# Layer-norm, attention and routed experts on one core: experts as one part between samples 15 and 16, dispatch and gathers inside the samples

## The reference

```
xn = _layernorm(x, axis=-1)
qkv = jnp.einsum('bsm,qhdm->bqhsd', x, W_qkv)           # 16 heads of 64
qk_rot = qk * cos + _rotate_half(qk) * sin               # first 32 of 64 dims
attn = softmax(where(causal, -inf, scores) / sqrt(DK))
probs = softmax(x @ router_w + router_b); top 2 of 9     # the ninth is a skip
h = gelu(einsum('btd,edf->ebtf', x, w1)); y = einsum('ebtf,efd->ebtd', h, w2)
x + attention(xn) + experts(xn)
```

## Time and profile before

| | |
|---|---|
| median of 3 runs | 1595.74 us (1595.12 to 1598.11) |
| span of the profiled execution | 1591.3 us |
| granted TensorE clock, mean | 0.924 |
| busy: PE, DVE, ACT, POOL | 1262.6, 1119.9, 1129.0, 985.1 us |

### The profile page before, as it was taken

One profiled execution on the slowest core, in us unless ns is written; L12 is line 12 of the kernel. 1 busy time (PEld: TensorE's weight loads), 2 busy tenths in 40 slices (PEclk: granted clock), 3 DMA queues, 4 the chain that ended last, 5 costly groups with the idle time before them and its releaser, 6 DMA issues.

```text
span 1591.3 us, 47515 instructions
## 1 busy us (share of the span) xinstructions
PE 1262.6 (79%) x13412; PEld 899.4 (57%) x13413; DVE 1119.9 (70%) x4292; ACT 1129.0 (71%) x3645; POOL 985.1 (62%) x1635
## 2 busy tenths in 40 slices
PE   2417989999899999999899999999859999567620
PEld 1304656666566666666566666666539899445520
DVE  5687787788877887788877887787647777345441
ACT  6407888888888888888888888888758888234310
POOL 3306888778877888778877888778640000544555
PEclk9658999999999999999999999999979999688765
DMA  9612233322332233322332233322422333222242
GB/s 288 166 39 56 61 76 89 74 62 60 87 89 62 62 69 88 81 62 60 85 87 65 61 67 86 83 64 60 115 81 81 84 88 86 66 79 76 75 132 65
DMA packets 121888, 131.83 MB, mean 83 GB/s; under 512 B 11568, under 2 KB 81456, under 8 KB 121520
## 3 DMA queue, kind: packets, MB, share of 16 engines
q1 hardware_dynamic: 113200, 113.41, 29.3%
q0 software_dynamic: 8576, 17.33, 3.8%
HBM read 29.89 MB, written 33.69 MB: 40 GB/s over the span
## 4 chain that ended last, share of the span: by engine, by line
PE 27%; POOL 20%; issue 19%; DVE 13%; DMA 10%; ACT 7%; DVEq 2%; another core or an unknown queue 1%; POOLq 0%; ACTq 0%; SPq 0%
DMA sorted_x_dram<-send_x,send_at 9%; PE bank L1056 6%; PE bank L1057 6%; PE bank L1058 6%; POOL probs L450 5%; POOL probs L451 4%; POOL arena L433 4%; ACT probs L597 3%; POOL arena L438 3%; PE bank L1127 2%; PE bank L1137 2%; PE bank L1151 2%; POOL arena L432 2%; PE bank L1186 1%; POOL sorted_x_dram L455 1%
## 5 line engine op out<-in xcount | busy, mean ns | idle before, releaser
L597 ACT ACTIVATE probs<-arena,neg_max 128x128 f32<-128x128 f32 (+1 forms) x1024 | 453.2, 446 | 94.7 <-DVE neg_max L910 77.3
L450 POOL TENSOR_TENSOR probs<-probs,inv_total 128x128 f32<-128x128 f32 x512 | 207.0, 404 | 184.8 <-DVE inv_total L917 127.9
L910 DVE CUSTOM_DVE_ANT_0 arena<-bank,causal 128x128 f32<-128x128 f32 (+1 forms) x1024 | 317.4, 348 | 0.0
L500 POOL DMA_INDIRECT arena<-sorted_y_dram,slots x128 | 123.3, 964 | 275.6 <-DMA sorted_y_dram<-arena 171.2
L1137 PE MATMUL bank<-ident,probs 128*128 128x128 f32 x1536 | 265.2, 282 | 13.0 <-POOL probs L451 4.7
L451 POOL TENSOR_SCALAR probs<-probs,inv_total 128x256 f32<-128x256 f32 x512 | 246.4, 481 | 0.0
L1137 PEld LDWEIGHTS bank<-ident,probs 128*128 128x128 f32 x1536 | 174.1, 142 | 83.5 <-issue 51.8
L597 ACT ACTIVATION_READ_ACCUMULATOR probs<-arena,neg_max 128x1 f32 x1024 | 195.2, 191 | 0.0
L578 ACT ACTIVATE probsT<-bank 128x384 f32<-128x384 f32 x384 | 184.4, 480 | 2.3 <-PE bank L1137 2.2
L928 DVE TENSOR_TENSOR arena<-bank,arena 128x256 f16<-128x256 f32 x256 | 107.3, 419 | 110.9 <-ACT arena L583 88.9
L1056 PE MATMUL bank<-xnT_lo,wqk_hi 128*128 (+1 forms) x512 | 143.7, 281 | 39.3 <-DVE arena L875 28.4
(11 more groups left out here) (155 smaller groups left out, 3378.5 us busy)
## 6 DMA issues: line engine op xcount, KB each, us to landing
second<-arena SPq DMA_DIRECT2D x128, 256.0 KB, 4.3
arena<-arena SPq DMA_DIRECT2D x128, 256.0 KB, 4.3
arena<-sorted_x_dram SPq DMA_DIRECT2D x80, 128.0 KB
sorted_y_dram<-arena SPq DMA_DIRECT2D x80, 128.0 KB
sorted_x_dram<-arena SPq DMA_DIRECT2D x3, 2560.0 KB, 20.1
arena<-experts_dram SPq DMA_DIRECT2D x8, 512.0 KB, 4.4
out_dram<-acc SPq DMA_DIRECT2D x16, 256.0 KB
sorted_x_dram<-arena SPq DMA_DIRECT2D x1, 2624.0 KB, 21.2
```

The source lines that it names most:

```text
L450: nc.gpsimd.tensor_tensor(p0, p0, inv_total[:, s % 4, 0:1].broadcast_to([P, P]), ALU.mult)
L597: last = nc.scalar.activation(probs[:, s % 4, at:at + w], masked[:, s % 2, at:at + w], ACT.Exp, bias=neg_max[:, s % 2, t:t + 1], scale=-1. ...
L910: last = nc.vector.tensor_tensor_reduce(out=masked[:, s % 2, at:at + w], in0=SC[s % 2][:, at:at + w], in1=causal[:, at:at + w], scale=1.0, ...
```

## The change

The sorted buffer has one part: 72 expert tiles instead of 80. The experts run between samples 15 and 16. Samples 0 to 15 send four tiles each (`PER`), by eight sends in steps `SEND_AT`, each still ahead of a wait for the one before; samples 16 to 31 gather and add the results of four tiles each (two of an earlier sample, two of their own), by eight gathers in steps `GATHER_AT` into a ring of four buffers (`stage`) and eight `combine`s in steps `COMBINE_AT`, and store two finished pairs of tiles each. The low parts of the rotary queries are taken on VectorE (`rope_low`), as those of the keys. Four of the eight experts' weights are loaded and split in the head (high parts on ScalarE, low parts on GpSimd by a scaling and a subtraction each), the other four around the end of sample 15. The owners of the expert tiles are found by one comparison and one sum instead of 14 small operations. Every engine's program now has two loops of samples with the expert loop between them. The core of the diff:

```diff
-PARTS = (44, 20)
+MID = B // 2
+PER = NT // MID
+EARLY = 4
 
 ET = 2 * P
-MAX_T = max(PARTS) * P // ET
-PART_T = [TOP * n * P // ET + E for n in PARTS]
-TILES = sum(PART_T)
-NS = E * len(PARTS)
+MAX_T = NT * P // ET
+TILES = TOP * NT * P // ET + E
...
-COMBINE_AT = PART_T[0] // BODY
-COMBINED = (0, 2, 2, 2)
-RING = sum(COMBINED)
+BACKS = 4
...
-SEND_AT = [1, 9, 12, 14]
+SEND_AT = [1, 3, 5, 7, 9, 11, 12, 14]
+GATHER_AT = [1, 3, 5, 7, 9, 10, 11, 13]
+COMBINE_AT = [3, 5, 7, 9, 11, 12, 13, 15]
...
+OPENING, FORMER, TURN, REOPEN, LATTER, FINAL = range(6)
+FILLS = (OPENING, REOPEN)
...
+        def former_samples(eng, body):
+
+
+            body(0, 0, OPENING)
+            with eng.Fori(0, MID // 2 - 1) as i:
+                body(2 * i + 1, 1, FORMER)
+                body(2 * i + 2, 0, FORMER)
+            body(MID - 1, 1, TURN)
+
+        def latter_samples(eng, body):
+
+            body(MID, 0, REOPEN)
+            with eng.Fori(MID // 2, B // 2 - 1) as i:
+                body(2 * i + 1, 1, LATTER)
+                body(2 * i + 2, 0, LATTER)
...
+            for e in range(EARLY):
+                load_expert(e)
...
+                if at == TURN:
+                    for r in range(GRP):
+                        sp.wait_ge(q_stacked[r], STACKED * (b + 2))
+                        sp.wait_ge(k_stacked[r], STACKED * (b + 2))
+                    for e in range(EARLY, E):
+                        load_expert(e)
+                if at in (REOPEN, LATTER, FINAL):
+                    store_former(b)
+                if at in (LATTER, FINAL):
...
+            def store_former(b):
+
+                u = b - MID
+                sp.wait_ge(combined, TOP * PER * u + TOP * TPS)
+                tiles_at = slice(TPS * u, TPS * u + TPS) if isinstance(u, int) else bass.ds(TPS * u, TPS)
+                sp.dma_start(out_tiles[:, tiles_at, :], acc[:, tiles_at, :]).then_inc(stored, 16)
...
-            def q_rope_low(j, m):
-                pool.wait_ge(rope_hi, ROPES * m + j + 1)
-                hi, lo = parts("rope", j)
-                nc.gpsimd.tensor_tensor(lo, roped[j], hi, ALU.subtract).then_inc(q_rope_lo, 1)
...
+            for e in range(EARLY):
+                pool.wait_ge(raw_hi, 4 + e)
+                nc.gpsimd.tensor_scalar(raw_e[e], raw_e[e], W_SCALE, 1.0, ALU.mult, ALU.mult).then_inc(early_scaled, 1)
+            for e in range(EARLY):
+                pool.wait_ge(early_scaled, e + 1)
+                nc.gpsimd.tensor_tensor(w_lo[:, e, :, :], raw_e[e].rearrange("p (k f) -> p k f", k=2), w_hi[:, e, :, :],
+                                        ALU.subtract).then_inc(early_low, 1)
...
+            def gather(k):
+
+                nc.gpsimd.indirect_dma_start(
+                    out=stage[:, k % BACKS, :], out_offset=None, in_=sorted_y[0:ROWS, :],
+                    in_offset=bass.IndirectOffsetOnAxis(ap=rows_at[:, k:k + 1], axis=0)).then_inc(gathered[k % BACKS], 16)
+
+            def sample(b, parity, at):
                 for s in range(H):
-                    if not first and s in SEND_AT:
-                        i = SEND_AT.index(s)
-                        if i == 0:
-                            pool.wait_ge(send_ready, b)
-                        else:
-                            pool.wait_ge(sent, 16 * (TPS * TOP * (b - 1) + i))
-                    if not (first and s < INV_LAG):
+                    sends = at in (OPENING, FORMER, TURN) and s in SEND_AT
+                    gathers = at in (REOPEN, LATTER, FINAL) and s in GATHER_AT
+                    if sends and s == SEND_AT[0]:
+                        pool.wait_ge(send_ready, b + 1)
+                    elif sends:
+                        pool.wait_ge(sent, 16 * (PER * TOP * b + SEND_AT.index(s)))
+                    if gathers:
+                        u, k = b - MID, GATHER_AT.index(s)
+                        if k == 0:
+                            pool.wait_ge(rows_ready, u + 1)
+                        if not (at == REOPEN and k < BACKS):
+                            pool.wait_ge(combined, TOP * PER * u + k - BACKS + 1)
+                    if not (at in FILLS and s < INV_LAG):
                         scale(16 * b + s - INV_LAG, s - INV_LAG)
-                    for kind, j, u, psum, n in beside(b, first, last, s - 3):
-                        if kind == "rope" and j < 2:
-                            q_rope_low(j, b + 1)
-                    for kind, j, u, psum, n in beside(b, first, last, s - 1):
+                    for kind, j, u, psum, n in beside(b, at, s - 1):
                         if kind == "rope":
                             rope_add(j, b + 1)
-                    if not first and s in SEND_AT:
+                    if sends:
                         send(SEND_AT.index(s))
...
+                    if gathers:
+                        gather(GATHER_AT.index(s))
...
+            former_samples(pool, sample)
+            rest_of(MID - 1)
+            for done in ys_out:
+                pool.wait_ge(done, 16 * TILES // 2)
+            latter_samples(pool, sample)
+            rest_of(B - 1)
...
+                if at == OPENING:
+                    act.wait_ge(early_low, EARLY)
...
+            former_samples(act, sample)
+            act.wait_ge(s_ready, 8 * MID)
+            for e in range(EARLY, E):
                 split_high(e)
+            rest_of(MID - 1)
 
             def xs_part(i, k):
...
-                step(nc.vector.memset(owner_f[0:1, :], 0.0))
-                for e in range(1, E):
-                    for h in range(len(PARTS)):
-                        own = owner_f[0:1, h * PART_T[0]:h * PART_T[0] + PART_T[h]]
-                        last = nc.vector.scalar_tensor_tensor(own, grid[0:1, 0:PART_T[h]], first_tile[0:1, e, h:h + 1], own,
-                                                              ALU.is_ge, ALU.add)
-                    step(last)
+                reached = scan[0][0:1, 0:TILES * (E - 1)].rearrange("p (n e) -> p n e", e=E - 1)
+                step(nc.vector.tensor_tensor(reached, grid[0:1, :].unsqueeze(2).broadcast_to([1, TILES, E - 1]),
+                                             first_tile[0:1, 1:E].unsqueeze(1).broadcast_to([1, TILES, E - 1]), ALU.is_ge))
+                step(nc.vector.reduce_sum(owner_f[0:1, :], reached, axis=AX.X))
...
             def dispatch(b):
 
                 if not (isinstance(b, int) and b == 0):
-                    dve.wait_ge(sent, 16 * TPS * TOP * b)
+                    dve.wait_ge(sent, 16 * PER * TOP * b)
+                for t in range(PER):
+                    tile = b * PER + t
+                    nc.vector.tensor_scalar(stage[:, t, :], row(acc, tile), row(neg_mean[:].unsqueeze(2), tile),
+                                            row(rstd[:].unsqueeze(2), tile), ALU.add, ALU.mult)
+                nc.vector.tensor_copy(rows_at[:].rearrange("p (t n) -> p t n", n=TOP), tile_slots(b * PER, PER)).then_inc(send_ready, 1)
+
+            def call_rows(b, at):
+
+                if at == REOPEN:
+                    dve.wait_ge(sent, 16 * TOP * NT)
+                former, own = (rows_at[:, 4 * i:4 * i + 4].rearrange("p (t n) -> p t n", n=TOP) for i in range(2))
+                nc.vector.tensor_copy(former, tile_slots((b - MID) * TPS, TPS))
+                nc.vector.tensor_copy(own, tile_slots(b * TPS, TPS)).then_inc(rows_ready, 1)
+
+            def combine(b, k):
+
+                u = b - MID
+                tile, n = (TPS * u if k < 4 else TPS * b) + k % 4 // TOP, k % TOP
+                dve.wait_ge(gathered[k % BACKS], 32 * u + 16 * (k // BACKS) + 16)
+                if n > 0:
+                    dve.wait_ge(combined, TOP * PER * u + k)
+                elif k >= 4:
+                    dve.wait_ge(mixed, b + 1)
+                a = row(acc, tile)
+                nc.vector.scalar_tensor_tensor(a, stage[:, k % BACKS, :], row(gates, tile)[:, n:n + 1], a,
+                                               ALU.mult, ALU.add).then_inc(combined, 1)
+
+            def mix(b):
+
                 for t in range(TPS):
                     tile = b * TPS + t
-                    if isinstance(tile, int):
...
-            def k_rope_low(j, m):
+            def rope_low(j, m):
                 dve.wait_ge(rope_hi, ROPES * m + j + 1)
                 hi, lo = parts("rope", j)
-                nc.vector.tensor_tensor(lo, roped[j % 2], hi, ALU.subtract).then_inc(k_rope_lo, 1)
+                nc.vector.tensor_tensor(lo, roped[j % 2], hi, ALU.subtract).then_inc(q_rope_lo if j < 2 else k_rope_lo, 1)
 
...
-                            k_rope_low(j, b + 1)
-                    if not (first and s < O_LAG) and (s - O_LAG) % 2 == 1:
+                            y_add(b - 1, j, u, psum, at in (FORMER, TURN))
+                    for kind, j, u, psum, n in beside(b, at, s - 3):
+                        if kind == "rope":
+                            rope_low(j, b + 1)
...
+                    if at in (OPENING, FORMER, TURN):
+                        if s == 0:
```

(29 more changed lines are left out.)

442 lines of the change are left out of this document (178 added, 264 removed).

## The result

The changed kernel takes 1608.4 us (median of 8 runs, 1598.8 to 1614.6) against 1595.95 us, ratio 1.0076 with a 95% interval of 1.0054 to 1.0099: 0.8% slower, where 3.5% faster was forecast. Its profiled execution took 1614.56 us with a span of 1612.7.

The account below looks back on a forecast made before the run. Bounds: GpSimd and VectorE in the rotary part, TensorE and equally long sends in the second, gathers at the end. From 1591.3 us, mainly -175.3 for experts, +93.4 and +22 for samples: 1537.4, with 4.4 to the median 1541.8; range 1490 to 1590.

Parts of the forecast that it names:

- 151 + 68 us more than the tiles need: Last two stretches of the kernel before: time spent beyond the tiles' own need, with tiles beside gathers taking 6.0 us.
- The saving of 175.3 us: Expert stage: eight tiles fewer and none beside a gather, 228.1 us in place of 403.4.
- Experts: Expert stage: 72 tiles at 3.04 us with GpSimd idle, handover down from 10.9 to 5.0 us.
- Samples 0 to 15: Eight sends instead of four: rotary part +1.4 us, second part +4.4, so 38.5 us a sample; +93.4 over sixteen.
- the chain of landings: Second part of samples 0 to 15: one more send waiting for a landing, +3.9 us, with `dispatch` +4.4, not hidden.
- Samples 16 to 31: Eight gathers and combines: 34.3 us a sample, bounds 32 and 38; VectorE waits about 1.5 us for step 9's gather.
- Meetings of GpSimd and VectorE: Samples 16 to 31: VectorE held up by GpSimd instructions at ten new meetings, 0.7 us a sample altogether.
- lock-out rival: Samples 16 to 31: the engines lock each other out, 0.8 us at each of ten meetings, 1657 us; chance 8%.
- The moved subtractions: Rotary part: two subtractions of 1.16 us leave GpSimd and come to VectorE at 0.69 us each.
- Ends: Sample 31 stays at 40.4 us plus 3 for the last store; the drain after sample 15 adds 7.7.
- Hidden sends: Rival: extra sends hide, samples 0 to 15 cost 1 us more each rather than 5.8, 1463 us; chance 12%.
- The clock did fall: Rival: TensorE's clock falls; at 0.65 its work would take 46 us a sample, 1660 us; chance 3%.

Follow-up runs that it names:

- x_after_p120: Changed kernel with 120 idle memsets at VectorE's start and 110 between the sample loops: 1575.1 us, 0.989 of the kernel before.
- x_scratch: Changed kernel with a sample's eight sends going to eight DRAM tensors, none waiting for another: 1543.2 us, 0.968 of the kernel before.
- x_after_again: Changed kernel without an edit, run again beside a kernel before of 1526.8 us: 1603.8 us, ratio 1.050.
- x_qlow_pool: Changed kernel with q's two rotary low parts moved back from VectorE to GpSimd: 1637.5 us, 1.027 of the kernel before.

## Why the prediction was wrong

The change made the kernel 0.8% slower where 3.5% faster was forecast. The mechanisms that the forecast named are there. The step that failed is the sum for a sample, 38.5 us before the experts and 34.3 behind them: it had no term for VectorE's own program at the loops' jumps, and the term for waits on gathers was too small. Experiments took away the first loop's waits and those for gathers, which gave 29 to 33 us and 22 us of the 67 us between 1541.8 and the median of 1608.4. The rest, 12 to 16 us, is about the size of the second loop's waits (16.1 us), which no run took away.

- **Bounds.** The stages are read rightly for the profiled execution, but "151 + 68 us more than the tiles need" counts the last stretch twice: 236 - 28 x 3.04 = 151 us is the whole, 83 in the stage of the 28 tiles and 68 behind it. The saving of 175.3 us is worked out without this slip. The loss of 151 us holds for the chip of that execution and not for every one: where the kernel before takes 1525 us, some 70 of them aren't there to be saved, and none of the kernels tried came below it.
- **Experts.** 230.0 us against 230.1, with GpSimd idle throughout. Right.
- **Samples 0 to 15.** The step "So a sample takes 32.7 + 1.4 + 4.4 = 38.5 us" is right without the jump: 38.2 in `x_after_p120`, whose parts are 19.4 (forecast 18.9) and 18.8 (19.4). `x_scratch` shows the chain of landings at 4.1 us (forecast 4.4). What failed is that the sum had no term for VectorE's program itself. A turn of its first loop has 350 instructions in place of 334 (64 reads of accumulators among them in both) and lies elsewhere. The wait of 2.7 to 3.0 us a turn and what follows it make 41.1 - 38.2 = 2.9 us a sample in the profiled execution, 2.0 in `x_after_again`, and 29 to 33 us by the medians. The waits themselves are only some 17.5 us of that. The clock stands at 0.95 with them and 0.99 without, and that this makes up the rest is an argument.
- **Samples 16 to 31.** "VectorE waits about 1.5 us for it, half of it in idle time" was too little: 53 us in 14 samples are 3.8 us each, and taking them away gives 1.4 us a sample. The waits at the jump are 16.1 us in 14 samples, 1.15 each. No run took these away, so that they cost their full length is an estimate from this trace. Together 2.5, and the sample missed its 34.3 by 2.6.
- **Meetings of GpSimd and VectorE.** The forecast took 0.7 us a latter sample, and none for a former one. What happens is a scaling of 0.94 us in place of 0.47 beside a subtraction, three times in the sample shown: 1.4 us on GpSimd's side. The other side, of which the forecast had no row, is in the combines: 42 of the 128 last over 0.45 us, all beside a GpSimd instruction that had begun before them. That adds 9 us in all, 0.6 a sample, far from the lock-out rival's 0.8 us at each of ten meetings:

```profile
L893 DVE SCALAR_TENSOR_TENSOR acc<-stage,gates,acc x128: 332/352/780, 1030.4 to 1601.9; 128x128 f32 x112, 128x128 f32<-128x128 f32 x16
```

- **The moved subtractions.** Costed as work on VectorE and relief for GpSimd, rightly: +0.3 us a sample alone, and 2.5 us a former sample won in the changed kernel (40.7 in `x_qlow_pool`, whose first loop has no wait at the jump, against 38.2 in `x_after_p120`).
- **Ends.** Sample 31 was 8 us cheaper than forecast. The 40.4 us taken over are those of a sample whose chain runs through its sends (24% of it is their landings, the last two 2.4 and 2.3 us, behind its last step); the changed kernel's has none there. No run tests this. Sample 15 with its drain cost 3.8 more.
- **The rivals.** Hidden sends: no, the chain's price was there. The clock did fall in the former samples, to 0.95 and not to 0.65, and stood at 0.99 in `x_after_p120` once VectorE's waits were gone.

## What to carry to other kernels

An edit that only adds or moves instructions can move a loop of another part of the program; look at the first instruction after each jump back, and at whether an instruction transfer falls into the wait ahead of it, before pricing the work; the count of transfers over the whole kernel shows only some of these waits. Put a few idle instructions ahead of a loop as a control. Where ten of them change the time by 3%, the place of the loop is a hidden term, and two versions compared at one place each are not yet compared. A saving that is read from one execution should be checked against the kernel before on another chip.

## What the runs showed of the hardware that was not expected

- Ten idle VectorE instructions at the program's start: 51 us (1524.1 to 1575.3); seven fewer: 1.056 down to 1.004.
- Of the places tried for the loops of 334 to 350 instructions a turn (accumulator reads among them), those that end where the loop of the kernel before does, or one instruction further, or 129 further, were free of the wait; ends 8 to 10, 40, 65, 212 and 213 further were not. That fits no rule on pieces of 128 or 256 instructions that these runs could settle. The loop of 386 instructions was free of it at none of the places seen. (The expectations give 414 and 450 for the two loops of the changed kernel; its trace has 350 and 386 a turn, 64 reads included.)
- GpSimd's scaling of 128x256 takes about 0.94 us where it begins while VectorE's 128x512 subtraction with two SBUF inputs is running (58 of the 61 long ones in the changed kernel), and 0.47 us where it began first (25 times).
- The identical program took 1593 to 1596 us in some sets and 1524 to 1527 in others, each within 0.4%. By its variants 65 of the 70 us lie between the first gather and the last, and 61.5 of these in the stage of expert tiles beside gathers. The changed kernel, with no tile beside a gather, took 1608.4 and 1603.8.
